# Expert gate and up products: 72 narrow-ended matmuls against 68 with a merged and a side-by-side chunk

## What is computed

```python
buf = zeros((E, C, D)).at[se, pos_c].add(where(valid, x[st], 0))
g = einsum('ecd,efd->ecf', buf, w_gate)
u = einsum('ecd,efd->ecf', buf, w_up)
eo = einsum('ecf,edf->ecd', silu(g) * u, w_down)
gathered = eo[se, pos_c] * (sw * valid)
y = zeros_like(x).at[st].add(gathered) + shared_swiglu(x)
```

## Time and profile before

| | |
|---|---|
| span of the profiled execution | 1742.8 us |
| median of three runs | 1743.47 us |
| attention | 0 to about 625 us |
| shared items | about 625 to 830 us |
| expert items | about 830 to 1689 us, 13.41 us a slot |
| tail of third blocks | about 1689 us to the end |

### The profile page before, as it was taken

One profiled execution on the slowest core, in us unless ns is written; L12 is line 12 of the kernel. 1 busy time (PEld: TensorE's weight loads), 2 busy tenths in 40 slices (PEclk: granted clock), 3 DMA queues, 4 the chain that ended last, 5 costly groups with the idle time before them and its releaser, 6 DMA issues.

```text
span 1742.8 us, 35871 instructions
## 1 busy us (share of the span) xinstructions
PE 1683.7 (97%) x11782; PEld 1533.6 (88%) x11782; DVE 1088.6 (62%) x2157; ACT 1030.9 (59%) x1875; POOL 771.8 (44%) x719
## 2 busy tenths in 40 slices
PE   4799999999999999999999999999999999999996
PEld 3588888888888888989999999999999999999995
DVE  7555566777677665343666666666666666666666
ACT  4557766665646452223566666666666666666665
POOL 6513212334323320242255555565555555655555
PEclk9889999999999999999999999999999999999998
DMA  5533433433322532312577777777777777777776
GB/s 199 168 102 94 115 112 94 116 91 108 93 82 80 179 110 87 123 38 89 184 231 227 213 210 231 220 212 211 230 220 211 207 224 227 217 209 222 236 199 184
DMA packets 148634, 287.71 MB, mean 165 GB/s; under 512 B 29230, under 2 KB 66350, under 8 KB 139328
## 3 DMA queue, kind: packets, MB, share of 16 engines
q1 hardware_dynamic: 115584, 236.05, 41.8%
q0 software_dynamic: 32960, 50.51, 13.9%
HBM read 241.83 MB, written 64.52 MB: 176 GB/s over the span
## 4 chain that ended last, share of the span: by engine, by line
PE 88%; issue 3%; ACT 3%; DVE 2%; POOL 1%; DMA 1%; POOLq 1%; DVEq 1%; ACTq 0%; SPq 0%
PE ps L2481 36%; PE ps L2499 19%; PE ps L1470 8%; PE ps L1478 5%; PE ps L1451 4%; PE ps L2458 4%; PE ps L1441 3%; PE ps L1467 2%; PE ps L1493 2%; PE ps L1426 1%; PE ps L2476 1%; PE ps L2822 1%; ACT prob L1138 0%; ACT L1138 0%; ACT L1199 0%
## 5 line engine op out<-in xcount | busy, mean ns | idle before, releaser
L2217 POOL DMA_INDIRECT out<-y,ids_s x128 | 206.5, 1614 | 302.6 <-issue 163.4
L2481 PE MATMUL ps<-xt_hi,gu_hi 128*128 128x256 f32 (+1 forms) x1856 | 303.5, 285 | 0.6 <-issue 0.6
L2481 PE MATMUL ps<-xt_lo,gu_hi 128*128 128x256 f32 (+1 forms) x1856 | 289.9, 278 | 0.0
L2481 PE MATMUL ps<-xt_hi,gu_lo 128*128 128x256 f32 (+1 forms) x1856 | 289.3, 278 | 0.0
L2256 DVE TENSOR_TENSOR gu_lo<-raw_gu,gu_hi 128x1408 fp32r<-128x1408 f32 (+2 forms) x132 | 214.5, 1625 | 112.4 <-ACT gu_hi L2253 108.1
L1138 ACT ACTIVATE prob<-ps 128x512 f32<-128x512 f32 x256 | 152.3, 597 | 185.0 <-PE ps L1451 172.7
L2481 PEld LDWEIGHTS ps<-xt_hi,gu_hi 128*128 128x128 f32 (+1 forms) x1856 | 250.6, 181 | 9.0 <-issue 2.9
L2481 PEld LDWEIGHTS ps<-xt_lo,gu_hi 128*128 128x128 f32 (+1 forms) x1856 | 244.5, 181 | 0.0
L2481 PEld LDWEIGHTS ps<-xt_hi,gu_lo 128*128 128x128 f32 (+1 forms) x1856 | 244.2, 181 | 0.0
L2197 POOL DMA_INDIRECT xg<-h_rows,ids_g x128 | 189.6, 1481 | 115.0 <-POOL ids_g L2192 50.6
L2313 ACT ACTIVATE h_hi<-h 128x256 fp32r<-128x256 f32 (+1 forms) x240 | 100.5, 419 | 223.9 <-DVE h L2382 221.1
(11 more groups left out here) (316 smaller groups left out, 3007.0 us busy)
## 6 DMA issues: line engine op xcount, KB each, us to landing
raw_gu<-in_w_gu SPq DMA_DIRECT2D x70, 1408.0 KB
raw_d<-in_w_d SPq DMA_DIRECT2D x70, 512.0 KB
raw_d<-in_w_d SPq DMA_DIRECT2D x70, 192.0 KB
qs<-qk_rows SPq DMA_DIRECT2D x192, 64.0 KB, 2.2
ks<-qk_rows SPq DMA_DIRECT2D x192, 64.0 KB, 2.1
xa<-in_x SPq DMA_DIRECT2D x16, 256.0 KB, 2.9
qk_rows<-k_hi SPq DMA_DIRECT2D x16, 256.0 KB, 2.2
qk_rows<-k_lo SPq DMA_DIRECT2D x16, 256.0 KB, 2.5
```

The costliest lines, as they stand in the source:

```text
L2217: pool.indirect_dma_start(out=out, out_offset=bass.IndirectOffsetOnAxis(B.ids_s[:, p, k:k + 1], 0), in_=B.y[:, p, k, :], in_offset=None, b ...
L2481: last = pe.matmul(gu_banks(it, c)[half], gu_columns(w, it, half, d, c), x[:, x_p, d, 0:W], start=i == 0, stop=i == len(steps) - 1)
```

## The change

The host lays the weights of each expert out anew, by contraction chunk: gate and up columns 0 to 127, gate and up 128 to 255, up and gate 256 to 319, gate and up 320 to 351. `gu_hi` gets 64 columns more for each contraction chunk, in which DVE writes the *low* parts of the last 32 + 32 columns (`last_parts`), next to their high parts. Chunk 2 of an expert item, 24 matmuls of 96 columns before, becomes:

- a *last* group of 8 matmuls with 128 weight columns (gate high, up high, gate low, up low, 32 each), by the high and by the low part of the rows, into PSUM bank 7. ACT copies the lower 64 result rows to SBUF (`last_copy`), DVE adds the upper 64 to them (`last_sum`);
- a *rest* group of 12 matmuls with 64 up and 64 gate columns merged, in chunk 2's bank.

Silu and mix of chunk 2 become two instructions each, one for the 64 and one for the 32 columns. The tail gets the same layout: 512 + 192 moving columns instead of 352 + 352, two silu and three mix instructions for each third block, and the first gate/up group waits for both halves of the weights' low parts. DMA sizes, shared items, attention and `down` stay; three semaphores of the attention phase are used again.

```diff
         else:
             eng.wait_ge(gu_hi.sem, gu_hi.value(it.weights, half + 1))
+            if half and not it.shared:
+                out, own, high = last_parts(B, p)
+                eng.tensor_tensor(out, own, high, ALU.subtract)
             eng.tensor_tensor(lo, raw, hi.bitcast(F32), ALU.subtract).then_inc(gu_lo.sem, 1)
...
+            if split_rest(it, c):
+                act.activation(B.sg[0:EX_REST, b, 0:W], rest_bank(c)[EX_REST:2 * EX_REST, :], ACT.Silu)
+                act.wait_ge(last_added.sem, last_added.value(it.expert, 1))
+                act.activation(B.last_rows[EX_LAST:2 * EX_LAST, 0, :], B.last_rows[0:EX_LAST, 1, :],
+                               ACT.Silu).then_inc(sg_ready.sem, 1)
+                return
...
+        def last_copy(it):
...
+            act.wait_ge(last_ready.sem, last_ready.value(it.expert, 1))
...
+            act.activation(B.last_rows[:, 0, :], last_bank[2 * EX_LAST:4 * EX_LAST, :],
+                           ACT.Copy).then_inc(last_copied.sem, 1)
...
             cut_d(act, it, True)
+            last_copy(it)
             silu(it, 2)
             high(it, 2)
...
+            if split_rest(it, c):
+                dve.tensor_tensor(B.h[0:EX_REST, b, 0:W], B.sg[0:EX_REST, b, 0:W], rest_bank(c)[0:EX_REST, :], ALU.mult)
+                dve.tensor_tensor(B.h[EX_REST:EX_REST + EX_LAST, b, 0:W], B.last_rows[EX_LAST:2 * EX_LAST, 0, :],
+                                  B.last_rows[EX_LAST:2 * EX_LAST, 1, :], ALU.mult).then_inc(h_ready.sem, 1)
+                return
...
+        def last_sum(it):
...
+            dve.wait_ge(last_copied.sem, last_copied.value(it.expert, 1))
+            dve.tensor_tensor(B.last_rows[:, 1, :], last_bank[0:2 * EX_LAST, :], B.last_rows[:, 0, :],
+                              ALU.add).then_inc(last_added.sem, 1)
...
             cut_d(dve, it, False)
+            last_sum(it)
             mix(it, 2)
             rest(it, 2)
...
+            elif split_rest(it, c):
+                both = [(x, d) for x in (B.xt_hi, B.xt_lo) for d in range(DC)]
+                for i, (x, d) in enumerate(both):
+                    last = pe.matmul(last_bank, last_columns(it, d), x[:, x_p, d, 0:W],
+                                     start=i == 0, stop=i == len(both) - 1)
+                last.then_inc(last_ready.sem, 1)
+                for i, (w, x, d) in enumerate(steps):
+                    last = pe.matmul(rest_bank(c), rest_columns(w, it, d), x[:, x_p, d, 0:W],
                                      start=i == 0, stop=i == len(steps) - 1)
...
     def silu(act, b):
         act.wait_ge(gate_up_turned.sem, gate_up_turned.value(b.j, 1))
-        act.activation(B.sg3, gate(b.p), ACT.Silu).then_inc(sg_ready.sem, 1)
+        act.activation(sg_wide, wide(b.p, 0), ACT.Silu)
+        act.wait_ge(gate_up_turned.sem, gate_up_turned.value(b.j, 2))
+        act.activation(B.sg3[:, 2 * P:F], narrow(b.p, *GATE_REST), ACT.Silu).then_inc(sg_ready.sem, 1)
```

More of the change, by code:

```diff
@@ L58 @@
 SH_REST = P // 2
+EX_REST = P // 2
+EX_LAST = F - 2 * P - EX_REST
+EX_COLS = 2 * F
+EX_HELD = EX_COLS + 2 * EX_LAST
+EX_WIDE = 4 * P
 TILES = NB * T
@@ L1922, in flat_gu, with held, by_chunk, last_parts @@
 def flat_gu(tensor):
-    return tensor[:].rearrange("p a b c f -> p (a b c f)")
+    return tensor.rearrange("p a n -> p (a n)")
+def held(tensor):
+    return tensor.shape[-1] // DC
+def by_chunk(ap, half):
+    return ap.rearrange("p (d n) -> p d n", d=DC)[:, 2 * half:2 * half + 2, 0:EX_COLS]
+def last_parts(B, p):
+    raw = B.raw_gu[:, p].rearrange("p a n -> p (a n)").rearrange("p (d n) -> p d n", d=DC)
+    hi = B.gu_hi[:, p].rearrange("p (d n) -> p d n", d=DC)
+    last = slice(EX_COLS - 2 * EX_LAST, EX_COLS)
+    return hi[:, :, EX_COLS:EX_HELD], raw[:, :, last], hi[:, :, last].bitcast(F32)
 def merged(it, c):
@@ L2025, in item_blocks @@
     sets = 3
-    XT0, GU0, Y0 = 0, 2, 5
+    XT0, GU0, Y0, LAST0 = 0, 2, 5, 7
     (gu_in, d_in, rows_in, added, gu_hi, gu_lo, d_hi, d_lo, xt_ready, xt_hi, xt_lo, gu_ready, sg_ready, h_ready,
@@ L2032, in item_blocks @@
     half_done, y_in, y_out, sh_rows_in = S.half_done, S.y_in, S.y_out, S.sh_rows_in
+    last_ready, last_copied, last_added = (Signal(A[n].sem, 1, first=TILES) for n in (
+        "v_prod_last_ready", "c_hi_last_copied", "c_lo_last_added"))
     rows_of = lambda dram, b: dram[b * W:(b + 1) * W, :].rearrange("(k p) n -> p k n", p=P)
@@ L2092, in gu_columns @@
         if not it.shared:
-            return tensor[:, it.half, half, d, o:o + m]
+            begin = d * held(tensor) + (2 * c + half) * P
+            return tensor[:, it.half, begin:begin + P]
         begin = gu_span(it, half)[0]
@@ L2105, in merged_columns, with rest_columns, last_columns, split_rest @@
         return flat_gu(tensor)[:, begin:begin + 2 * SH_REST]
+    def rest_columns(tensor, it, d):
+        begin = d * held(tensor) + EX_WIDE
+        return tensor[:, it.half, begin:begin + 2 * EX_REST]
+    def last_columns(it, d):
+        begin = (d + 1) * EX_HELD - 4 * EX_LAST
+        return B.gu_hi[:, it.half, begin:begin + 4 * EX_LAST]
+    def split_rest(it, c):
+        return not it.shared and c == NF - 1
+    def rest_bank(c):
+        bank = ps[:, GU0 + c % sets]
+        return bank[0:2 * EX_REST, 0:W]
+    last_bank = ps[0:4 * EX_LAST, LAST0, 0:W]
     def chunk(item, c, back):
@@ L2246, in cut_gu @@
         begin, end = gu_span(it, half)
-        hi, lo = flat_gu(B.gu_hi)[:, begin:end], flat_gu(B.gu_lo)[:, begin:end]
-        raw = B.raw_gu[:].rearrange("p q a n -> p (q a n)")[:, begin:end]
+        if it.shared:
+            hi, lo = flat_gu(B.gu_hi)[:, begin:end], flat_gu(B.gu_lo)[:, begin:end]
+            raw = B.raw_gu[:].rearrange("p q a n -> p (q a n)")[:, begin:end]
+        else:
+            hi, lo = by_chunk(B.gu_hi[:, p], half), by_chunk(B.gu_lo[:, p], half)
+            raw = B.raw_gu[:, p, half].rearrange("p (d n) -> p d n", d=2)
         if act:
@@ L2303, in silu @@
                 act.wait_ge(h_ready.sem, h_ready.value(j.e, n + 1))
-            act.activation(B.sg[0:m, (it.half * NF + c) % 2, 0:W], gu_banks(it, c)[0], ACT.Silu).then_inc(sg_ready.sem, 1)
+            b = (it.half * NF + c) % 2
+            if split_rest(it, c):
[4 more added lines that the diff above has]
+                return
+            act.activation(B.sg[0:m, b, 0:W], gu_banks(it, c)[0], ACT.Silu).then_inc(sg_ready.sem, 1)
+        def last_copy(it):
+            if it.shared:
+                return
+            act.wait_ge(last_ready.sem, last_ready.value(it.expert, 1))
+            if not it.known or it.e > SH_ITEMS:
+                act.wait_ge(h_ready.sem, h_ready.value((it - 1).e, NF))
+            act.activation(B.last_rows[:, 0, :], last_bank[2 * EX_LAST:4 * EX_LAST, :],
+                           ACT.Copy).then_inc(last_copied.sem, 1)
         def high(it, c):
@@ L2476, in gate_up @@
                     last = pe.matmul(ps[:, GU0 + c % sets, 0:W], merged_columns(w, it, d), x[:, x_p, d, 0:W],
+                                     start=i == 0, stop=i == len(steps) - 1)
+            elif split_rest(it, c):
[6 more added lines that the diff above has]
+                    last = pe.matmul(rest_bank(c), rest_columns(w, it, d), x[:, x_p, d, 0:W],
                                      start=i == 0, stop=i == len(steps) - 1)
@@ L2599, in xt, with wide, narrow @@
         return B.xt_hi[:, p, :, 0:P], B.xt_lo[:, p, :, 0:P]
[L2601 to L2605, removed]
+    def wide(p, which):
+        return ps[:, (2, 4)[p], :].rearrange("p (c g n) -> p c g n", c=2, g=2)[:, :, which, :]
+    def narrow(p, a, z):
+        return ps[:, (3, 7)[p], a:z]
+    GATE_REST = (EX_REST, 2 * EX_REST + EX_LAST)
+    UP_REST, UP_LAST = (0, EX_REST), (2 * EX_REST + EX_LAST, 2 * (EX_REST + EX_LAST))
+    sg_wide, h_wide = (t[:, 0:2 * P].rearrange("p (c n) -> p c n", c=2) for t in (B.sg3, B.h3))
     def turned_h(p, c):
@@ L2727, in act_gu @@
             act.wait_ge(gu_in[b.p].sem, gu_in[b.p].value(b.turn, 16))
-        act.activation(B.gu_hi[:, b.p, half], B.raw_gu[:, b.p, half].rearrange("p (c f) -> p c f", c=DC),
+        act.activation(by_chunk(B.gu_hi[:, b.p], half), B.raw_gu[:, b.p, half].rearrange("p (d n) -> p d n", d=2),
                        ACT.Copy).then_inc(gu_hi.sem, 1)
@@ L2769, in dve_gu @@
         dve.wait_ge(gu_hi.sem, gu_hi.value(b.j, half + 1))
-        dve.tensor_tensor(B.gu_lo[:, b.p, half], B.raw_gu[:, b.p, half].rearrange("p (c f) -> p c f", c=DC),
-                          B.gu_hi[:, b.p, half].bitcast(F32), ALU.subtract).then_inc(gu_lo.sem, 1)
+        dve.tensor_tensor(by_chunk(B.gu_lo[:, b.p], half), B.raw_gu[:, b.p, half].rearrange("p (d n) -> p d n", d=2),
+                          by_chunk(B.gu_hi[:, b.p], half).bitcast(F32), ALU.subtract).then_inc(gu_lo.sem, 1)
     def dve_x(dve, b):
@@ L2785, in mix @@
         dve.wait_ge(sg_ready.sem, sg_ready.value(b.j, 1))
-        dve.tensor_tensor(B.h3, B.sg3, up(b.p), ALU.mult).then_inc(h_ready.sem, 1)
```

(18 more changed lines are left out.)

14 lines of the change are left out of this document (10 added, 4 removed).

## The result

The changed kernel takes 1812.67 us, the median of four runs (1811.57 to 1813.3), against 1743.87 us before on the same chip: a ratio of 1.0393, 95% interval 1.038 to 1.0406. The forecast was 1808 us with a range of 1790 to 1825. The profiled execution after took 1812.34 us, of which the span is 1810.5 us.

The account below looks back on a forecast made before the run. The ACT-DVE chain was to become the bound at 14.42 us a slot, over TensorE's 12.94. Span 1742.8 + 63 (items) + 1.4 (tail) = 1807, plus 0.7 for the median: 1808 us, range 1790 to 1825.

Parts of the forecast that it names:

- the closed chain through ACT and DVE: Expert slot: ACT and DVE release each other in a ring needing 12.84 us, 0.57 under TensorE's 13.41.
- TensorE's part: Chunk 2 of an expert slot: four fewer matmuls save 0.47 us, making TensorE's own slot 12.94 us.
- Steps 1 to 6: Added ACT and DVE instructions and waits in an expert slot: +1.58 us on the chain, copy and 64-column silu hidden.
- The second mix: DVE, behind the down weights: splitting chunk 2's mix into two instructions adds 0.34 us.
- The stall: TensorE ahead of the second two transposes: waits for `xt_lo`, 1.48 us a slot, some 60 times.
- TensorE busy some 30 us less: Sign on TensorE's busy time: some 30 us less if the forecast is right.
- Items: The 64 expert items: each slot grows 1.01 us, less 1.5 once, together +63 us.
- tail: End of the kernel: later silu and added instructions cost +1.4 us, 0.5 to 3.
- TensorE stays the bound: Expert slots: added instructions fall in idle time, slot 12.94 us, total 1715 us; chance 0.08.
- Half of it: Expert slots: shorter handovers, say 0.8 of 1.58 us, give a chain of 13.64 and 1759 us; chance 0.06.
- The clock falls: TensorE in expert slots: stalls lower its granted clock, 14.64 us a slot, 14 us more, 1822; chance 0.06.
- Less than it says: Chunk 2: 20 wide matmuls take as long as 24 narrow ones; would not move the forecast; no chance given.

Follow-up runs that it names:

- the three subtractions: Kernel before plus three unused 128x256 DVE subtractions ahead of the second low part of each expert's weights: 1763.72 us, ratio 1.0109.
- the two runs that differ in it: Changed kernel minus copy, sum, silu and mix of the last 32 columns, with `last_parts` (1733.74 us) and with it for the first experts only (1712.86 us).
- without the last columns' steps: Changed kernel with copy, sum, silu and mix of the last 32 columns taken out, `last_parts` and all matmuls kept: 1733.74 us, ratio 0.9938.
- the other order: Changed kernel with `last_copy` moved ahead of chunk 1's high part of h and `last_sum` ahead of the down weights' low parts: 1760.53 us.
- the last kernel: Changed kernel with both calls moved, a signal for each down high part, and low parts copied a slot later: 1710.6 us, ratio 0.9808.

## Why the prediction was right, point by point

**What bounds the kernel.** That the closed chain through ACT and DVE decides, and not their busy share, is shown by the three subtractions: both engines well under three quarters busy, and 1.01 us more work on one of them costs 18.7 us. Its size was slightly off: 0.57 of slack as the wait in the earlier trace rows reads, 0.69 by the run.

**TensorE's part.** Predicted 0.47 us saved a slot. The 20 matmuls of chunk 2 take 1212.36 - 1209.99 = 2.37 where 24 took 2.90: 0.53. A group of four with 128 columns takes 1211.00 - 1210.55 = 0.45, one with 96 before took 1214.71 - 1214.24 = 0.47, so the assumption of equal pace was a little too careful. TensorE's own slot is 12.84, not 12.94.

```profile
1210.55 0.62 PE L2568 MATMUL ps<-xt_lo,gu_hi 128*128 128x256 f32 x4
1211.00 0.62 PE L2572 MATMUL ps<-xt_hi,gu_hi 128*128 128x256 f32 x4
```
```profile
1214.24 0.63 PE L2481 MATMUL ps<-xt_hi,gu_hi 128*96 128x256 f32 x4
1214.71 0.63 PE L2481 MATMUL ps<-xt_lo,gu_hi 128*96 128x256 f32 x4
```

**Steps 1 to 6.** `last_parts`: 0.34 predicted, and 20.9 / 64 = 0.33 by the two runs that differ in it. The copy and the silu of the 64 columns hide, as predicted: ACT still idles 1.54 behind them, ahead of the silu of the 32 columns. Sum, 0.60 behind the second low part: 1215.51 - 1214.91 = 0.60. Silu, 0.45: 0.44. First mix, 0.45: 0.45. High part of h, 0.45: 0.45. Two terms were mis-sized. The second mix was put at 0.34, like a second instruction of a kind, and took 0.43: it starts only when the first has ended, 1216.40 + 0.41. And the results copy follows the high part of h by 1217.73 - 1217.28 = 0.45, where the chain had 1212.25 - 1211.93 = 0.32 with three subtractions; I had no term for it. It too starts only when the instruction before it has ended, 1217.28 + 0.42; with three subtractions it starts 0.10 ahead of that end. All kernels made from the changed one have the 0.44 or 0.45, those without the last columns too, so it is not a handover of the change.

The two have one thing in common. By the code, each starts on other partitions than the last instruction of its engine that read or wrote the same memory: the second mix reads from partition 32 and writes from 64, behind a mix at 0; the copy reads PSUM from partition 0, behind a silu that read it from 64. Two runs have such a pair with the same two instructions, a high part of the down weights and the silu of the 64 columns, which reads PSUM from partition 64. With the other order, ACT's last read of PSUM before the silu was from 64 too (`last_copy`); without the last columns' steps it was from 0. In this order, on ACT:

```profile
1208.14 0.62 ACT L2326 ACTIVATE d_hi<-raw_d 96x512 fp32r<-96x512 f32 x1
1208.66 0.37 ACT L2363 ACTIVATE sg<-ps 64x256 f32<-64x256 f32 x1
```
```profile
1210.46 0.61 ACT L2326 ACTIVATE d_hi<-raw_d 96x512 fp32r<-96x512 f32 x1
1211.10 0.38 ACT L2363 ACTIVATE sg<-ps 64x256 f32<-64x256 f32 x1
```

The silu follows by 0.52 in the first and by 0.64 in the second. So an instruction that starts on other partitions costs some 0.1 us more in all these rows; no run varied the partitions alone, so that they are the reason is likely and not shown. Sum: 12.72 + 1.58 + 0.09 + 0.13 = 14.52. The forecast of 14.42 had three small errors: the base 0.12 too high, the steps 0.09 and 0.13 too low. That they partly cancel is luck.

**The stall.** Predicted 1.48 ahead of the second two transposes, behind `xt_lo`, some 60 times. It is there, 61 times, marked 1.32 in the mean. By starts the stall is larger: the last group ahead of it starts at 1206.12 and takes 0.45, the transposes start at 1208.07, 1.50 later. And they take 1208.59 - 1208.07 = 0.52 after the stall instead of 1209.99 - 1209.64 = 0.35. Together that is 1.50 + 0.17 = 1.67, and 14.50 - 12.84 = 1.66. That is also why the forecast of "TensorE busy some 30 us less" failed: it is 1683.7 - 1666.1 = 17.6. Of the 64 x 0.53 = 34 us saved, about 61 x 0.35 = 21 come back as time in which TensorE is recorded as busy while it waits; the last 4 or 5 I did not follow.

**Items, tail, rest.** Items +63 predicted, +68.2 measured; tail +1.4 predicted, +2.6 measured, within its bounds of 0.5 to 3. But the same stretch takes 56.6 to 58.5 us in the four kernels without the change and 57.5 to 59.2 us in the six with it, so much of the 2.6 can be a difference between executions, and what the change costs in the tail is not shown. The stretch ahead of the items is 3.1 us shorter after, and the change does not touch it; over all ten kernels it ends at 633.0 to 637.5 us, so this too is a difference between executions. The median lies 2.2 us over the span, where I took 0.7; each of the nine other profiled executions whose time is on record took 1.7 to 1.8 us more than its span. So the miss of 4.7 us is 5.2 from the items, 1.2 from the tail, 1.5 from this last step and 3.1 back from the front. That the front gave 3.1 back is luck.

**The rivals.** *TensorE stays the bound*, 1715: not what happened, but it is what the changed matmuls are worth once the chain is no longer than TensorE's 12.84, at 1710.6 and 1712.86. *Half of it* falls: the handovers were as long as the rows said, or longer. *The clock falls*: the granted clock is 1.00 over all of the items after, with 61 stalls of 1.3 us; not one of the rows bears it out. *Less than it says* falls with the 0.53.

The Trainium skill, page TensorEngine Tiling (Array Packing), section PSUM Bottleneck, warned that a faster TensorE leaves moving results out of PSUM as it was. In the changed kernel the saving is lost, as it warns: 0.53 us saved on TensorE, a slot 1.09 longer. But reads of PSUM are not what decided: the last kernel has the same ones and keeps the saving. The steps that decided stand between SBUF and SBUF as much as at PSUM, and cost by waiting in turn. For the Trainium skill, page TensorE: Matmul & The Clock Gate, section "A second HAM failure mode: psum-queue depth-cycling", the result is that stalls of 1.3 us once in 14.5 us left the clock alone here.

## What to carry to other kernels

Where two helper engines release each other, follow the releases once round and add up the starts: the room of both is the one wait in that ring that an outside engine ends, here 0.57 us as marked and 0.69 by experiment, and not their idle share. Price an added instruction by its place, as here: 0.34 us behind a like one, 0.43 where it started on other partitions than that, some 0.45 for each change of engine, nothing in a gap. If a saving is lost that way, look first at the order and at signals that cover more than their reader needs: the same work went from 1812.67 to 1760.53 by two moved calls, and to 1710.6 by a signal for each part and a copy that was moved into a gap.

## What was not expected of the hardware

A busy TensorE is no proof that it is the bound. With three subtractions it is recorded as busy for 856.78 of 857 us, at a slot of 13.73 where its work needs 13.41: a stall of 0.3 us a slot does not show as idle time. The waits of ACT and DVE for TensorE tell it better: with three subtractions there are none from 900 to 1650 us, and in the last kernel, where TensorE is the bound, ACT's silus wait for it 107 times. The results copy alone does not tell it, as it waits in neither. And narrower weights gave no faster matmul: four of 96 columns 0.47 us, four of 128 columns 0.45.
